# Log-polar convolution with batch norm: the middle products copied and gathered in their own image's second half

## What is computed

```python
xp = log_pooling(x)            # 12 bins: averages over pixels of a 9x9 window, as 12 "taps"
out = conv(xp, w_conv1, (BH, BW), 'VALID')
out = out + conv(x, w_center, (1, 1), 'VALID') + b_center[None, :, None, None]
mean = out.mean(axis=(0, 2, 3), keepdims=True)
var = out.var(axis=(0, 2, 3), keepdims=True)
out = (out - mean) * rsqrt(var + EPS) * gamma[...] + beta[...]
return relu(out + x)
```

## Time and profile before

| what | value |
|---|---|
| median of three runs | 1686.37 us (1686.28 to 1686.71) |
| the profiled execution | 1686.6 us |
| its span, first to last instruction | 1684.8 us |
| PE busy | 1489.2 us, 88% |
| DVE busy | 1531.3 us, 91% |
| ACT busy | 645.3 us, 38% |
| mean granted clock of PE | 0.949 of 2.4 GHz |
| loop over the images, about | up to 1531 us of the span |
| tail of loads and stores | the last 150 us, 382 to 425 GB/s |

### The profile page before, as it was taken

How to read it: one execution, slowest core, us unless ns; L and a number is a source line. 1 busy time by engine, 2 the same in 40 slices (tenths; PEclk the granted TensorE clock), 3 DMA queues, 4 the chain that set the end, 5 groups by cost and what they waited for, 6 DMA issues and landing times.

```text
span 1684.8 us, 21919 instructions
## 1 busy us (share of the span) xinstructions
PE 1489.2 (88%) x8468; PEld 1476.5 (88%) x8468; DVE 1531.3 (91%) x1455; ACT 645.3 (38%) x689; POOL 2.7 (0%) x21
## 2 busy tenths in 40 slices
PE   6899999999999999999999999999999999993000
PEld 6899999999999999999999999999999999993000
DVE  8999999999999999999999999999999999995423
ACT  3234343343333434334333343433433334434423
POOL 0000000000000000000000000000000000000000
PEclk8999999999999999999999999999999999997555
DMA  2010111001111011100111101111011110149999
GB/s 110 20 38 29 38 38 38 21 27 38 38 38 38 29 38 38 38 29 19 38 38 38 38 29 38 38 38 37 11 38 38 38 38 29 38 159 421 425 424 382
DMA packets 28615, 129.54 MB, mean 77 GB/s; under 512 B 3520, under 2 KB 3520, under 8 KB 28608
## 3 DMA queue, kind: packets, MB, share of 16 engines
q1 hardware_dynamic: 23744, 103.77, 17.0%
q10 hardware_dynamic: 4864, 25.69, 3.7%
HBM read 78.88 MB, written 50.58 MB: 77 GB/s over the span
## 4 chain that ended last, share of the span: by engine, by line
PE 50%; DVE 27%; issue 11%; SPq 5%; ACT 4%; DMA 3%; DVEq 0%; ACTq 0%
PE acc L625 17%; PE acc L627 16%; PE acc L626 16%; DVE pooled_split L403 6%; DVE pooled L402 6%; DVE inner_split L403 5%; SPq L266 3%; ACT inner_split L324 3%; DVE box L402 2%; DVE y_stage L402 2%; DVE row L402 2%; DMA phase<-x 2%; SPq L263 2%; DMA out<-phase 1%; ACT phase L394 0%
## 5 line engine op out<-in xcount | busy, mean ns | idle before, releaser
L334 ACT ACTIVATE pooled_split<-pooled 128x1456 fp32r<-128x1456 f32 x192 | 273.4, 1425 | 608.0 <-DVE pooled L402 608.0
L403 DVE TENSOR_TENSOR pooled_split<-pooled,pooled_split 128x1456 fp32r<-128x1456 f32 x192 | 317.4, 1667 | 0.3 <-ACT pooled_split L334 0.3
L625 PE MATMUL acc<-inner_split,w_first 128*128 128x406 f32 (+1 forms) x640 | 225.7, 353 | 36.3 <-DVE y_stage L402 25.0
L625 PE MATMUL acc<-pooled_split,w_first 128*128 128x364 f32 x768 | 253.6, 330 | 2.4 <-DVE pooled_split L403 2.4
L625 PE MATMUL acc<-pooled_split,w_outer 128*128 128x364 f32 x768 | 252.3, 329 | 1.1 <-DVE pooled_split L403 1.1
L626 PE MATMUL acc<-pooled_split,w_first 128*128 128x364 f32 x768 | 252.6, 329 | 0.0
L627 PE MATMUL acc<-pooled_split,w_first 128*128 128x364 f32 x768 | 252.5, 329 | 0.0
L626 PE MATMUL acc<-pooled_split,w_outer 128*128 128x364 f32 x768 | 252.2, 328 | 0.0
L627 PE MATMUL acc<-pooled_split,w_outer 128*128 128x364 f32 x768 | 251.8, 328 | 0.0
L627 PE MATMUL acc<-inner_split,w_first 128*128 128x406 f32 (+1 forms) x640 | 222.8, 348 | 0.0
L625 PE MATMUL acc<-inner_split,w_inner 128*128 128x406 f32 (+1 forms) x640 | 221.2, 346 | 1.1 <-DVE inner_split L403 1.1
(11 more groups left out here) (82 smaller groups left out, 2200.7 us busy)
## 6 DMA issues: line engine op xcount, KB each, us to landing
x_pad<-x SPq DMA_DIRECT2D x64, 392.0 KB, 3.3
y_dram<-y_stage SPq DMA_DIRECT2D x31, 784.0 KB, 5.0
phase<-y_dram SPq DMA_DIRECT2D x30, 784.0 KB, 28.3
phase<-x SPq DMA_DIRECT2D x30, 784.0 KB, 30.5
out<-phase ACTq DMA_DIRECT2D x30, 784.0 KB, 16.0
w_stage<-w_raw SPq DMA_DIRECT2D x2, 896.0 KB, 7.7
out<-x_pad ACTq DMA_DIRECT2D x2, 784.0 KB, 20.4
w_stage<-w_raw SPq DMA_DIRECT2D x2, 768.0 KB, 9.1
```

The costliest lines, as they stand in the source:

```text
L334: nc.scalar.activation(view(pooled_split, 2 * j * PAIR, (1, PAIR)), view(pooled, (PAIRS * c + j) % 2 * PAIR, (1, PAIR)), ACT.Copy)\
L403: sub = lambda out_, a, b: nc.vector.tensor_tensor(out_, a, b, ALU.subtract)
L625: nc.tensor.matmul(place, hi_w, hi_in, start=start, stop=False)
```

## The change

`copy_m1(image)` is called by ACT in half 1 of its own image, between the second and the third `split_pooled`, instead of at the head of the next image. `take_middle(image)` is called by DVE in half 1 of its own image, between the low parts of the second and third pooled planes, instead of in half 0 of the next image. The two calls after the loops, for the last image, go. The functions themselves, and what they wait for, are as before; PE, SP and POOL are unchanged.

```diff
@@ ACT: image_steps
                 for c in range(CH):
                     s = CH * image + c
-                    if c == 0 and not first:
-                        copy_m1(image - 1)
                     split_inner(s)
...
                     for j in range(PAIRS):
                         split_pooled(s, c, j)
+                        if c == 1 and j == 1:
+                            copy_m1(image)
...
                 image_steps(image)
-            copy_m1(LAST)
             for o in range(CH):
                 measure(LAST, o)
@@ DVE: image_steps
                         lo_of_weights(c, range(INNER_GROUPS))
-                    if c == 0 and not first:
-                        take_middle(image - 1)
...
                     lo_of_pooled(s, c, 1)
                     if c == 0 and not first:
                         take_y(image - 1)
+                    if c == 1:
+                        take_middle(image)
                     lo_of_pooled(s, c, 2)
...
                 image_steps(image)
-            take_middle(LAST)
             take_y(LAST)
```

## The result

The changed kernel takes 1822.24 us, median of four runs (1821.55 to 1823.18), against 1686.36 us for the kernel before, measured beside it: ratio 1.081, 95% interval 1.079 to 1.082. The profiled execution has a span of 1821.4 us. The prediction was 1821.5 us, with a range of 1767 to 1829. It is 8% slower, and the case put down as likeliest, a longer chain and a falling clock, is the one that came.

What follows compares the result with a forecast made beforehand. Bound: a loop through PE, ACT and DVE, 46.72 us per image. Span 1684.8 + 84.1 (chain) + 1 (tail) + 50 (clock) = 1820, plus 1.6 = 1821.5 us; range 1767 to 1829.

Steps and rivals of the forecast that it cites:

- the case put down as likeliest: In the image loop, a longer chain and a clock falling in nearly every image: 1821 us, chance 0.68.
- What bounds the kernel: A loop through PE, ACT's `split_inner` and DVE to `take_y` sets 46.72 us per image; PE idles 0.54 us.
- rival C: Gather in the first half makes `take_y` late; without it PE loses its 0.54 us wait: 16 us, to 1670; chance 0.02.
- Steps 1 and 2: ACT's copy cannot start before 23.39 us of an image; DVE's moved gather waits 2.43 us for it, until 24.25.
- Step 3: New loop through copy, gather, last low part and `take_y`: 49.51 us per image instead of 46.72, +2.79.
- Step 4: First images: PE starts image 2 3.15 us late; with 29 periods of 2.79 following, 84.1 us.
- Step 5: Tail of loads and stores shifts whole; loads released 4.1 us later add 1 us, between 0 and 4.1.
- Step 6: PE's clock falls in 28 of 30 gaps of 3.33 us, each slowing half 0's D/V products by 1.79: 50 us.
- The range: The forecast's own range: 1800 us (20 falls of 30, less 1 of tail) to 1828 (30 falls, tail 4).
- Rival A: In the loop, the wait arises but PE's clock stays up: 1771.4 us, chance 0.19.
- Rival B: No new DVE wait at the gather, only changed order, products being done: 10 us, to 1696; chance 0.04.
- Rival D: PE's clock stays low longer after each gap; one more us in each of 30 images gives +15, to 1836; chance 0.07.

Runs made afterwards that it cites:

- the filled gap: Changed kernel plus 30 useless 100-column products on TensorE per image, ahead of the middle products of half 0: 1777.3 us, ratio 1.054.
- the run with thin products on both sides: Changed kernel plus 12 useless 100-column products ahead of the middle products and 12 after PE's wait for `take_y`: 1858 us once, 1893 to 1899 in three.

## Why the prediction was right, point by point

- **What bounds the kernel.** Right as to the loop (the run with the early `take_y`). Wrong in one number: "PE therefore works 46.18 us per image" is 45.95, as a wait costs 0.23 us more than is shown. It cancels in the difference of the two kernels, which both have one wait, but rival C's price would have been some 24 us, not 16.
- **Steps 1 and 2.** Right: copy at 23.39 us (24.94 less the clock's 1.55), DVE's wait 2.52 us against 2.43. The term "0.86" for copy to gather measured 1.04: it was read from the last image, whose gather stands behind the loop, and gathers inside the loop take 0.18 us more.
- **Step 3.** +2.79 per image, and measured without the clock 49.69 − 46.72 = +2.97, the 0.18 more of the step before.
- **Step 4.** Image 2 was forecast 3.15 us late and was 2.47 late (139.28 against 136.81). The first product of the convolution also started 0.94 us sooner than in the profile before (17.82 against 18.76), ahead of all that the change touches; this offset was not in the sum. With it the shift is 3.41, 0.26 more than forecast.
- **Step 5.** The shift of PE's start of image 31 is 1624.94 − 1491.78 = 133.2 us, and the span grew by 136.6. So the tail took 3.4 us more. Of this 1.6 is the low clock of the last image, which is inside the forecast's 50; the other 1.8 fits the late release of the loads, before which the queues ran dry (the row below: DMA share 0.38, 85 GB/s). I took 1 of a bound of 0 to 4.1.

```profile
1654.00:1656.00 2.00, 2.00 (x14) 2.00 (x14) 0.30 (x1) 0.00 (x0) 0.00 (x0) 1.00 0.38 85
```

- **Step 6.** Right that the clock falls nearly every time and that the D/V products pay for it; the reason given was wrong. "A gap of 3.33 us reaches past 2.3" takes a fall 2.3 us into a gap for a rule. In the changed kernel the falls came 3.4 to 4.2 us after PE ran dry, more than half of them after work had come back, and gaps shorter than 2.3 us lost the clock too. The step was right by a number that happened to lie on the right side, so the forecast of the clock is in part luck. The size: 28 falls at 1.79 = 50 us were 30 falls at 1.5 to 1.6, 44.9 us by the filled gap. Against these 5 us too many stand 6 too few in the chain and the tail (90.9 against 85), 5 of them the 0.18 of step 2. That 1821.5 met 1822.2 so closely is luck too; each term is within 7 us.
- **The range.** Its lower end is mis-added: 20 falls at 1.79 with no tail give 1686.4 + 84.1 + 36 = 1806 us, not 1800.
- **Rival A** did not come (its case, the chain without the falls, is the run with 30 added products: 1777 us against its 1771). The gap came out at 3.50 us and the clock fell 30 times. By the Trainium skill ("TensorE: Matmul & The Clock Gate", section "HAM oscillation — how this bites in real kernels") this length is just past the point above which an idle gap costs the clock. The measurements go below that point: gaps of 2.16 and 2.83 us lost the clock in every image, and 1.92 in 5 to 27 of 30. Here the measurement decides: idle time well under the figure of the Trainium skill costs the clock when it comes back each period.
- **Rival B** did not come, as nothing brought the middle products forward; the rival put in words what would have been needed. **Rival C** did not come. The runs do not test it by itself, as each that takes the gather out of the first half also puts a wait into the second; what speaks against it is still that ACT waits 3.43 us for PE ahead of `split_inner`. **Rival D** did not come in the changed kernel, but such longer low stretches exist: in 4 of 30 falls with the copy alone, and in 21 of 29 in the run with thin products on both sides.

## What to carry to other kernels

Moving a consumer earlier is worth nothing before its producer is there: look up in the timeline when the producer ends in the period, and compare it with when the consuming engine reaches the new place. If the engine gets there first, its wait can pull what is queued behind it into the critical chain; here it did, on DVE behind the gather and on ACT behind the copy. A repeated idle gap on TensorE had a second price beside its length, the low clock: from 2.2 us up in nearly every image, here half as much again, and at 1.9 us in 5 to 27 of 30. And the cheap cure for the original wait lay elsewhere, in `take_y` one instruction sooner (1686.4 to 1662.2 us).

## What was unexpected of the hardware

- At a fixed idle time of 1.92 us per period, the number of falls of TensorE's clock went from 5 to 16 to 27 of 30 as the period grew from 48.1 to 48.8 and 49.7 us (as without a fall).
- The falls kept 51.20 us apart in kernels whose periods were 51.14 and 51.25 us, and slipped against the gaps until one gap of 3.40 us passed without a fall.
- Products of 100 columns took 0.109 us each, against 0.167 us for 364 columns.
- An idle time of 0.54 us shown ahead of a product cost 0.77 us of the period.
- The same hand-over from ACT to DVE took 0.86 us outside the loop and 1.04 us inside it. With the wait that ends last put behind the two others it took 0.93 us inside, but 0.96 outside.
